# A fused adapter, attention and feed-forward kernel: its first stage in another order, and each weighted sum in one run

## The reference

```python
hidden = gelu(x @ down_W.T + down_b)                       # (8, 512, 64)
hidden = hidden @ expert_W[idx].T + expert_b[idx] + domain_emb[idx]
x = layernorm(hidden @ up_W.T + up_b + x) * ln_gamma + ln_beta
scale, shift = split(silu(sin_emb(timestep)) @ W_ada + b_ada)
x = layernorm(x) * (1 + scale) + shift
q, k, v = x @ Wq + bq, x @ Wk + bk, x @ Wv + bv            # 16 heads of 16
scores = where(mask, -inf, q @ k.T / 4 + bias)             # bias (8, 16, 512, 512)
x = x + (softmax(scores) @ v) @ Wo + bo
h = layernorm(x) * g2 + beta2
return x + gelu2(h @ W1 + b1) @ W2 + b2                    # gelu2(a) = a sigmoid(1.702 a)
```

## Time and profile before

| | us |
|---|---|
| median of 3 runs (lowest to highest) | 978.33 (977.5 to 978.37) |
| the profiled execution | 975.33 |
| its span, from the first to the last instruction | 973.4 |
| TensorE busy in the span | 904.8 (93%) |
| VectorE busy | 720.6 (74%) |
| ScalarE busy | 702.2 (72%) |
| GpSimd busy | 704.1 (72%) |

### The profile page before, as it was taken

The page is one execution under the profiler, slowest core; times in us unless marked ns, Lnnn a source line. Parts: engine busy times, 40 slices in busy tenths (PEclk is TensorE's granted clock), DMA queues, the critical chain, the costliest instruction groups (busy, mean ns, idle before and its releaser), DMA issues.

```text
span 973.4 us, 20669 instructions
## 1 busy us (share of the span) xinstructions
PE 904.8 (93%) x6472; PEld 652.3 (67%) x6472; DVE 720.6 (74%) x1905; ACT 702.2 (72%) x1661; POOL 704.1 (72%) x407
## 2 busy tenths in 40 slices
PE   4648979999999999999999999999999999999986
PEld 1435545777677776777777776777777777677765
DVE  5738787878778787878778787878778787675642
ACT  2237758978788787878788787878788787877641
POOL 2448966888779886888769877878688886885700
PEclk8777989999999999999999999999999999999998
DMA  5499858876897669876797768876897668865300
GB/s 170 130 286 319 268 151 237 252 227 200 243 287 214 209 207 247 254 223 206 223 290 216 225 205 253 246 218 207 236 278 204 204 203 248 247 200 154 115 12 11
DMA packets 147948, 207.39 MB, mean 213 GB/s; under 512 B 14385, under 2 KB 62322, under 8 KB 147842
## 3 DMA queue, kind: packets, MB, share of 16 engines
q1 hardware_dynamic: 147842, 206.09, 71.7%
HBM read 185.05 MB, written 20.99 MB: 212 GB/s over the span
## 4 chain that ended last, share of the span: by engine, by line
PE 77%; DVE 2%; issue 2%; POOL 1%; ACT 1%; DVEq 0%; POOLq 0%; ACTq 0%
PE tp L834 19%; PE pv L791 12%; PE la L754 11%; PE sc L827 11%; PE lc L739 10%; PE lb L591 4%; PE lb L771 3%; PE lb L607 2%; DVE xm L1091 1%; PE lc L573 1%; POOL bias_s L494 1%; PE la L581 1%; PE la L565 1%; PE lb L565 1%; PE pv L802 1%
## 5 line engine op out<-in xcount | busy, mean ns | idle before, releaser
L494 POOL TENSOR_TENSOR bias_s<-mask_f,bias_s 128x1024 f32<-128x1024 f32 x256 | 602.3, 2371 | 159.6 <-DMA bias_s<-in_bias 159.0
L1360 DVE CUSTOM_DVE_ANT_0 bias_s<-sc,bias_s 128x512 f32<-128x512 f32 x512 | 349.1, 684 | 178.7 <-PE sc L827 166.1
L974 ACT ACTIVATE bias_s<-bias_s,mx 128x512 f32<-128x512 f32 x512 | 371.4, 726 | 115.9 <-DVE mx L1360 113.9
L834 PE MATMUL tp<-ident,bias_s 128*128 128x128 f32 x2048 | 311.6, 275 | 6.1 <-ACT pT L980 3.1
L834 PEld LDWEIGHTS tp<-ident,bias_s 128*128 128x128 f32 x2048 | 253.0, 142 | 87.3 <-issue 17.0
L980 ACT COPY pT<-tp 128x512 f32<-128x512 f32 x336 | 195.7, 583 | 91.2 <-PE tp L834 90.9
L827 PE MATMUL sc<-stk,stq 128*128 128x512 bf16 x512 | 197.3, 386 | 24.9 <-DVE mx L1360 20.4
L791 PE MATMUL pv<-pT,v_all 128*32 128x256 f32 x2048 | 138.4, 388 | 0.2 <-issue 0.2
L754 PE MATMUL la<-w_s,act_s 128*128 128x256 f32 x512 | 128.2, 380 | 0.2 <-DVE act_s L1317 0.2
L1367 DVE COPY pT<-tp 128x512 f32<-128x512 f32 x176 | 120.5, 684 | 4.3 <-PE tp L834 4.2
L739 PE MATMUL lc<-hT,w_s 128*128 128x256 f32 x464 | 120.8, 384 | 2.3 <-ACT hT L929 1.9
(11 more groups left out here) (172 smaller groups left out, 809.9 us busy)
## 6 DMA issues: line engine op xcount, KB each, us to landing
bias_s<-in_bias SPq DMA_DIRECT2D x256, 512.0 KB, 4.4
stq<-q_parts SPq DMA_DIRECT2D x128, 96.0 KB, 3.8
stk<-k_parts SPq DMA_DIRECT2D x128, 96.0 KB, 4.1
k_parts<-kb SPq DMA_DIRECT2D x32, 192.0 KB, 2.3
q_parts<-qb SPq DMA_DIRECT2D x32, 192.0 KB, 2.5
xT<-in_x_t SPq DMA_DIRECT2D x8, 512.0 KB, 6.2
k_parts<-kb SPq DMA_DIRECT2D x32, 128.0 KB, 2.3
stq<-q_parts SPq DMA_DIRECT2D x64, 64.0 KB, 4.0
```

Source lines behind the costliest of these rows:

```text
L494: pool.tensor_tensor(tile, mask_f[:, :, :], tile, ALU.subtract).then_inc(s["masked"], 1)
L834: last = pe.transpose(tp[n % 2][:, kt * P:(kt + 1) * P], bias_s[:, n // 2 % NB, n % 2, kt * P:(kt + 1) * P], ident[:, :])
L974: act.activation(tile, tile, ACT.Exp, bias=mx[:, t:t + 1], scale=-1.0, accum_out=sums[:, j, head_of(hh):head_of(hh) + 1]).then_inc(s["prob ...
L1360: dve.tensor_tensor_reduce(out=tile, in0=sc[t % 2][:, :], in1=tile, scale=1.0, scalar=BIG, op0=ALU.add, op1=ALU.min, accum_out=mx[:, t:t + ...
```

## The change

- SP's first loads are in another order: the loads for the norm, the weights of keys, queries and values and two biases go to ScalarE's queue, and the seven other experts come on SP before the embedding's rows.
- The seven experts are prepared, turned and folded right after the first adapter products, before norms are finished. The embedding's product and the forming of its rows (`modulation`) come after the turning of the seven experts; the adapter of batch 1 is done before the rows of chunk 0 are turned. ScalarE instead of VectorE spreads and copies the folded experts, and takes the function tables in the order gelu, sine, exponential, gelu, exponential.
- Both key chunks are projected and split before the first queries. The keys' stores are counted for each half of the heads, and the first group's key stack is loaded by chunk as soon as its half is stored (`load_half_keys`). Chunk 0's queries are stored and their first group is loaded on ScalarE's queue.
- The W1 constants and the eight identity products move from the second iteration to the end of the first stage.
- Each weighted sum is one run of 32 products, at slots 14.6, 22.6, 30.6 and 6.6.
- The statistics of the second norm wait for the residual sum and no longer for ScalarE's copy, which comes after them. In the last chunk two more tiles (29 and 31) are moved by VectorE.

```diff
-             pv=((14.0, 15.0), (22.0, 23.0), (30.0, 31.0), (6.0, 7.0)), spread=(23.3, 7.3))
+             pv=(14.6, 22.6, 30.6, 6.6), spread=(23.3, 7.3))
...
+LAST_DVE_MOVES = DVE_MOVES + (29, 31)
...
-MID = dict(wo=(21.0, 21.6), x2=22.6, copy=23.0, st2=23.6, mv2=24.3, hn=27.0, ht=28.6)
+MID = dict(wo=(21.0, 21.6), x2=22.6, st2=23.6, mv2=24.3, copy=25.0, hn=27.0, ht=28.6)
...
-W1_AT = dict(parts=4.6, diag=(5.6, 12.0, 13.3, 14.6), sums=(18.0, 19.0), scale=(20.3, 21.3), lift=(22.0, 23.0))
+W1_AT = dict(sums=(18.0, 19.0), scale=(20.3, 21.3), lift=(22.0, 23.0))
...
+            def load_half_keys(b, g, e):
                 wait(sp, s["sc_ready"], TI * (2 * b - 1) + TG * (g + 1))
-                sp.wait_ge(s["k_out"], 64 * (2 * b + 2))
+                sp.wait_ge(k_out[g % 2], 32 * (2 * b + e + 1))
...
@@ SP @@
-            load("ada_in", [(w_ada_s, w_ada.rearrange("(c p) n -> p c n", p=P)),
-                            (ada_r, b_ada.to_broadcast([B, 2 * D]))])
             load("up_in", [(up_w[0:A], upT), (up_w[A:A + 1], up_b)])
             sp.wait_ge(s["idx_ready"], 1)
             load_expert(0, "expert0_in")
             load_x(0)
-            load("norm_in", ...)
             load_x(1)
-            load("k_w_in", ...)
-            load("q_w_in", ...)
-            load("v_w_in", ...)
-            load("b2_in", [(b2_r[:, :], b2.to_broadcast([P, D]))])
+            load("ada_in", ...)
+            for b in range(1, B):
+                load_expert(b, "experts_in")
+            load_xt(1)
             sp.wait_ge(s["emb_ready"], 1)
             load("emb_out", [(emb_d, emb_s)])
-            load_xt(1)
             sp.wait_ge(s["emb_out"], 16)
             load_mod(0)
-            for b in range(1, B):
-                load_expert(b, "experts_in")
+            load("b2_in", [(b2_r[:, :], b2.to_broadcast([P, D]))])
             load_mask(0)
             load_bias(0)
             load_bias(1)
             store_keys(0)
-            store_queries(0)
+            load_half_keys(0, 0, 0)
             store_keys(1)
-            load_queries(0, 0)
-            load_keys(0, 0)
+            load_half_keys(0, 0, 1)
             load_x(2)
...
@@ TensorE @@
             turn_experts(0, 1, "turned0")
-            embedding()
             pe.wait_ge(s["up_in"], 32)
             pe.wait_ge(s["spread0"], 1)
             fold_expert(0, tp[1], 0).then_inc(s["fold_sum"], 1)
             pe.wait_ge(s["folded"], 1)
             adapter_up(0)
             adapter_up(1)
+            pe.wait_ge(s["eff"], 1)
+            turn_experts(1, B, "turned")
+            embedding()
+            pe.wait_ge(s["spread"], 1)
+            fold_expert(1, tp[1], 1)
...
+            pe.wait_ge(s["folded"], 2)
+            adapter_down(1, 0)
+            adapter_down(1, 1)
             turn_rows(0)
+            turn_rows(1)
             pe.wait_ge(s["k_w_in"], 16)
             pe.wait_ge(s["a_xt1"], 1)
             keys(0, 0)
             keys(0, 1)
-            turn_rows(1)
+            pe.wait_ge(s["a_xt1"], 2)
+            keys(1, 0)
+            keys(1, 1)
             pe.wait_ge(s["scaled"], 1)
             pe.wait_ge(s["emb_ready"], 1)
             queries(0, 0)
             queries(0, 1)
...
-                    for kt in range(2 * half, 2 * half + 2):
+                    for kt in range(KT):
...
@@ ScalarE @@
+            act.wait_ge(s["vec_in"], 64)
+            load("norm_in", ...)
+            load("k_w_in", ...)
+            load("q_w_in", ...)
+            load("v_w_in", ...)
+            adapter_gelu(0)
             act.wait_ge(s["idx_ready"], 2)
             act.activation(sm[:, 12, :], sm[:, 11, :], ACT.Sin).then_inc(s["setup_act"], 1)
             act.wait_ge(s["setup_act"], 1)
             act.activation(sm[:, 13, :], sm[:, 12, :], ACT.Exp, scale=-1.0).then_inc(s["setup_act"], 1)
-            act.wait_ge(s["vec_in"], 64)
-            adapter_gelu(0)
+            act.wait_ge(s["turned"], 1)
+            act.copy(ew_t[0:A, 1:B, 0:A], pv[0:A, A:B * A].rearrange("p (b o) -> p b o", o=A)).then_inc(s["spread"], 1)
...
+            act.wait_ge(s["fold_sum"], 2)
+            act.copy(fold[:, 1, :], tp[1][0:A + 1, D:2 * D])
...
+            adapter_gelu(1)
+            act.activation(sm[:, 13, :], sm[:, 12, :], ACT.Exp, scale=-1.0)
             copy_rows(0)
+            copy_rows(1)
             keys(0, 0)
...
+            act.wait_ge(s["d_q"], 1)
+            for m in range(2):
+                act.dma_start(q_d[0, m].rearrange("n p t -> p n t"), qb[:, :, m * CH:(m + 1) * CH]
+                              ).then_inc(s["q_out"], 16)
...
@@ VectorE @@
             effective(0, 1, "eff0")
-            gate_embedding()
+            turns_of_angles()
             dve.wait_ge(s["turned0"], 1)
-            spread(0, 1, "spread0")
-            modulation()
+            dve.tensor_copy(ew_t[0:A, 0, 0:A], pv[0:A, 0:A]).then_inc(s["spread0"], 1)
...
             add_residual(0)
             add_residual(1)
+            gate_embedding()
             first_stats(0)
             first_mean(0)
             first_stats(1)
             first_mean(1)
+            dve.wait_ge(s["experts_in"], 16 * (B - 1))
+            effective(1, B, "eff")
             center(0)
             center(1)
+            modulation()
             normalize(0)
...
-            dve.wait_ge(s["experts_in"], 16 * (B - 1))
-            effective(1, B, "eff")
             key_parts(0, 0)
             key_parts(0, 1)
+            key_parts(1, 0)
             query_parts(0, 0)
+            key_parts(1, 1)
             query_parts(0, 1)
-            key_parts(1, 0)
-            key_parts(1, 1)
...
             values(0)
+            shift_parts()
+            for ft in range(FT):
+                ins = dve.tensor_scalar(b1_diag[:, ft, :], ident[:, :], vec[:, VEC["b1"] + ft:VEC["b1"] + ft + 1],
+                                        None, ALU.mult)
...
                     if at == when["st2"]:
-                        dve.wait_ge(s["a_x2"], m + 1)
+                        dve.wait_ge(s["d_x2"], m + 1)
```

More of the change, by code:

```diff
@@ L121, in on_act @@
 def on_act(n):
-    return n % TI not in DVE_MOVES
+    return n % TI not in (LAST_DVE_MOVES if n // TI == NCH - 1 else DVE_MOVES)
 def moved(n, by_act):
-    return sum(on_act(k) == by_act for k in range(n % TI)) + n // TI * (21 if by_act else 11)
+    return sum(on_act(k) == by_act for k in range(n))
 def head_of(hh):
@@ L312, in build @@
         stk_in = [sem(f"stk_in{g}") for g in range(NG)]
+        k_out = [sem(f"k_out{m}") for m in range(2)]
         block = ctx.enter_context(nc.Block())
@@ L641, in _ @@
             adapter_up(1)
+            pe.wait_ge(s["eff"], 1)
[3 more added lines that the diff above has]
+            fold_expert(1, tp[1], 1)
+            for b in range(2, 4):
+                fold_expert(b, sc[1], b % 2)
+            for b in range(4, 6):
+                fold_expert(b, lb, b % 2)
+            for b in range(6, 8):
+                last = fold_expert(b, lc, b % 2)
+            last.then_inc(s["fold_sum"], 1)
+            pe.wait_ge(s["folded"], 2)
+            adapter_down(1, 0)
+            adapter_down(1, 1)
             turn_rows(0)
+            turn_rows(1)
             pe.wait_ge(s["k_w_in"], 16)
@@ L793, in weigh @@
                                              stop=(g % 2 == 1 and kt == KT - 1), tile_position=(0, 32 * h))
-                    if half == 1:
-                        last.then_inc(s["pv_done"], 1)
+                    last.then_inc(s["pv_done"], 1)
                 def spread_inverses(r):
@@ L880, in keys @@
                     act.wait_ge(s["p_k"], c + 1)
-                    wait(act, s["k_out"], 64 * (c - 1))
+                    wait(act, k_out[0], 32 * (c - 1))
+                    wait(act, k_out[1], 32 * (c - 1))
                     for mt in range(2):
@@ L889, in keys, with load @@
                     act.copy(kb[c % 2][:, 1, :], k_bank(c)[:, :]).then_inc(s["a_k1"], 1)
+            def load(sem_name, pairs):
+                for dst, src in pairs:
+                    act.dma_start(dst, src).then_inc(s[sem_name], 16)
+            act.wait_ge(s["vec_in"], 64)
+            load("norm_in", [(gamma_r[:, :], gamma.to_broadcast([P, D])), (beta_r[:, :], beta.to_broadcast([P, D]))])
+            load("k_w_in", [(wk_s[:, :, :], wk.rearrange("(c p) n -> p c n", p=P))])
+            load("q_w_in", [(wq_s[:, :, :], wq.rearrange("(c p) n -> p c n", p=P))])
+            load("v_w_in", [(wv_s[:, :, :], wv.rearrange("(c p) n -> p c n", p=P)),
+                            (bo_r[:, :], bo.to_broadcast([P, D])), (bv_r[:, :], bv.to_broadcast([P, D]))])
+            adapter_gelu(0)
             act.wait_ge(s["idx_ready"], 2)
@@ L1291, in w1_steps @@
                 def w1_steps(t):
-                    if t in W1_AT["diag"]:
-                        for ft in range(2 * W1_AT["diag"].index(t), 2 * W1_AT["diag"].index(t) + 2):
-                            ins = dve.tensor_scalar(b1_diag[:, ft, :], ident[:, :],
```

(5 more changed lines are left out.)

105 lines of the change are left out of this document (41 added, 64 removed).

## The result

The changed kernel takes 969.5 us (median of 4 runs, 969.18 to 970.35) against 977.91 beside it (977.11 to 978.37); the ratio is 0.9916, 95% interval 0.9899 to 0.9933. So it is 8.4 us faster, where 18.6 were forecast. The profiled execution took 970.35 us with a span of 968.5.

What follows compares the result with a forecast made beforehand. TensorE was taken to bound the middle, VectorE the second iteration, and a chain over all engines and the DMA queue the first stage. -12.9 - 7.3 + 2.2 - 0.6 = -18.6 gave 959.7 us, range 951 to 971.

Steps and rivals of the forecast that it cites:

- rival 2: Weighted-sum merges save nothing because TensorE then waits for maxima or probabilities it used to find ready: 972.6 us, chance 0.12.
- rival 1: First stage costs more, as clock, table changes and the lock add up: +8 instead of +2.2, 965.5 us, chance 0.17.
- merged sums: Weighted sums, about 200 to 920 us: one run instead of two saves TensorE 0.243 us each, 53 x 0.243 = 12.9.
- W1 in the first stage: Second iteration, 120 to 140 us: moving W1's preparation off VectorE leaves TensorE's 12.7 us as the bound, gaining 7.3 us.
- first stage: Before the first score: the embedding behind the experts delays the modulation rows; key loads end at 52.7 instead of 50.46, +2.2 us.
- the end: Last chunk: its statistics no longer wait for ScalarE's copy, which takes 948.68 to 949.30 off the chain, -0.6 us.
- rival 4: Second iteration: W1 work does not leave the path; GpSimd's pace or bias loads replace it, 4 us less gained, 963, chance 0.08.
- upper end, +5.5: First-stage cost if TensorE is still at the slow clock at the last adapter product and key projection, table changes queued behind.
- port rule: GpSimd and VectorE share an exclusively locked port pair; expert preparation could be held, 1.8 us more, not included in the sum.

Runs made afterwards that it cites:

- each alone: Changed kernel with one first-stage edit: batch 1's adapter product and gelu later, 969.89 us; or the embedding's product ahead of turning the experts, 968.99 us.
- both together: Changed kernel with the embedding's product ahead of turning the experts and batch 1's adapter product and gelu behind the rest: 966.07 us, ratio 0.9907.

## Why the prediction was half wrong

Two steps failed: that all 53 merges keep their 0.24 us, and that the new first stage costs 2.2 us. The measured 969.5 us lies inside the forecast's wide range of 951 to 971, but this says nothing for the sum: most of rival 2 and rival 1 came together, which the prediction priced nowhere; W1's larger gain made up for a part of it.

| term | forecast | the part alone, by medians |
|---|---|---|
| merged sums | -12.9 | -4.1 |
| W1 in the first stage | -7.3 | -10.9 |
| first stage | +2.2 | +6.7 |
| the end | -0.6 | -0.7 |
| sum | -18.6 | -9.0 |

**Merged sums: this term failed.** The surplus of a run, 0.24 us, was read rightly: with the fourth group at slot 6.0 four merges save 0.90 an iteration. What failed is the step from the run to all 53 merges. "VectorE and ScalarE both have 20% to spare" is an average over the stage; at slots 4 to 6 there is no other work of TensorE, and the old run at 6.0 was the cover for the maximum of slot 4. Rival 2 named this wait and placed it behind the run. It lies before it, at one of the four places only, and takes 0.65 of the 0.97.

The Trainium skill (TensorEngine Tiling (Array Packing), Key Properties) says that a change of tiling mode drains TensorE. The trace is in line with it, though it does not show the drain itself: entering and leaving a run of 32-column products costs 0.24 us, and four runs fewer save 0.90 us an iteration where no wait takes their place.

**W1: mechanism right, size somewhat too small.** The eight identity products take 1.66 us together and the waits of 3.87 and 2.61 us are gone. With W1 moved alone TensorE is busy for 19.0 of the 20 us from 120 to 140, so no other engine took over, and rival 4 is out. Iteration 1 takes 61.1 to 62.2 us in the four profiles with this work in it and 51.5 to 54.1 in ten without it and with the bias tiles in their old place; it is 9.6 us shorter with this edit alone and 7.5 to 8.7 shorter from the new first stage alone (61.6) to the kernel after (54.1 and 52.9). The forecast, 7.3, looked only at TensorE from 120 to 140 us, while the constants stand ahead of this stretch and the last pairs behind it. How much of the spread comes from the way the bias tiles arrive around it is not settled.

**The first stage: this term failed, and rival 1 came true, near its price of 8.** The cost is 6.7 us alone and 5.1 by the old first stage with the rest of the change. The chain by the forecast's own stations, in the profile after:

| | forecast | profile |
|---|---|---|
| second residual add | 17.2 | 20.7 |
| experts prepared | 22.7 | 26.0 |
| end of the embedding's product | 27.2 | 30.5 |
| modulation rows there | 33.9 | 36.6 |
| first key part | 41.3 | 48.0 |
| last key part | 46.3 | 53.0 |
| first score | 54.6 | 62.6 |

The first 3.5 us come from the start: expert 0 was ready at 11.78, the angle instructions now stand behind it, and the upward products took 2.07 and 1.91 us, 1.7 more than before, for which 1.3 had been put. The preparation itself took the 2.1 forecast, and up to the modulation rows 0.8 of the 3.5 was regained. The next 4.0 are the adapter product, its gelu and the table change, ahead of the turned rows on TensorE and ScalarE: the sum had put transposes and a copy right behind the ready rows and these steps at nothing. The last 1.3 are on SP: the second store waits for three loads. The forecast had a slow TensorE at the adapter product and at the key projection, with the table changes behind, as its upper end, +5.5; the product was slow in the profiled execution (3.67 us), the key projection was not (1.96), and the first score still came 10.2 us later.

Of these 10.2 us, 3.0 come back in iteration 0 (54.3 instead of 57.3), whose length hangs on the bias tiles; the forecast said that nothing would be given back. This rests on one pair of profiles: the kernel after measured again gives back 0.4. Over all profiles, iteration 0 ends 4 to 11 us later with the unchanged new first stage (six, at 114.8 to 120.5) than with the old one (five, at 109.3 to 111.1), 7.3 by the means, which fits the 6.7.

Expert 0 was issued at 6.28, 0.4 us sooner than before, and was there at least 1.2 us later than the 10.6 at which VectorE used it before, while ScalarE's queue moved 1.3 MB. The Trainium skill (DMA: Bandwidth & Descriptors, Issuing engines are not separate DMA queues) says that DMAs of several engines interleave on the same sixteen and that a second queue saves only issue time. The later landing is in line with it; no run separates this from SP's own loads.

By the port rule of the Trainium skill that the prediction cited, the experts' preparation could have been held by GpSimd's roots, +1.8. It was not: 0.59, 0.62, 0.17 and 0.62 us. The one root beside it took 1.07 instead of 0.69: it started at 24.66, 0.10 us behind an instruction of VectorE, and GpSimd was the one held here.

**The end: right.** The statistics moved up by the 0.6; the interval of the part alone reaches to no change, so the size rests on the trace.

What stays open: why one program's first stage falls into the one or the other pattern of TensorE's clock, which moves its first score by some 3 us, and how much of the first stage's 6.7 each of its edits has. An order with both chunks' key stores ahead of the half loads was not tried.

## What to carry to other kernels

Work that looks like overhead between two short steps can be the cover of a wait. Before merging runs, look at what stands between the neighbours afterwards, place by place: of 0.24 us saved four times, two thirds were taken back at one of the four places, and moving that run by 0.6 of a slot recovered them. In a first stage look not only at when the first product can start but at which loads the first iteration waits for, and use the idle DMA engines for them: that was worth 6 us here, more than the merges as first placed. Two steps in series have to be moved together: here each alone showed nothing (969.9 and 969.0 us), and both together brought the first score forward by 5 to 8 us.

## What was not expected of the hardware

- TensorE's pace differs between executions of one program in a stage of short bursts: four folds take 1.03 or 1.91 us, the adapter product 2.54 or 3.67. In the profile after, the clock column reads 1.00 from 30 to 44 us although these instructions take their longer durations, and so it does at the first adapter product of both kernels (3.65 us from 7.25 and 7.48 us on, against 1.93 later). The durations are nearly double, as the level of 1.2 GHz would give; a column of 1.00 ahead of its first lower reading is no proof of the full clock.
- Three bare slots of 0.65 us (a score and four transposes) in a row are too fast for a maximum of 0.68 and an exponential of 0.72 us, even where these engines are busy for only 78 and 80% of the stage.
- The DMA engines were full (share 1.04, 332 GB/s) in the first iteration of a kernel whose mean share is 0.78 in the middle.
